# A graph network kernel: every 40th tile of gathered rows is fetched from another queue

## What is computed

```python
x = _layernorm(x + L0(...))    # msg = (x @ weight[r])[edge_type, src];  segment_sum(msg, dst)
x = _layernorm(x + L1(...))    # mean over edges of x[src], two products, row norm, batch norm, relu
x = _layernorm(x + L2(...))    # three attention layers: softmax over a node's edges, then the weighted sum
x = _layernorm(x + L3(...))    # segment_sum((x @ W)[src] * norm, dst)
```

## Time and profile before

| what | value |
|---|---|
| median of 3 runs | 6719.5 us |
| profiled execution, its span | 6723.0 us |
| a0, from barrier to barrier | 995.0 us, at 385.5 to 1380.5 |
| a1 | 987.6 us, at 1380.5 to 2368.1 |
| a5 | 994.8 us, at 5728.2 to 6723.0, the end |
| POOL busy in the three | 741.9, 740.6 and 741.0 us |
| PE busy in the three | 740.0, 764.1 and 684.0 us |
| mean of one gather on POOL | 947 to 948 ns |

### The profile page before, as it was taken

How to read it: one execution, slowest core, us unless ns; L and a number is a source line. 1 busy time by engine, 2 the same in 40 slices (tenths; PEclk the granted TensorE clock), 3 DMA queues, 4 the chain that set the end, 5 groups by cost and what they waited for, 6 DMA issues and landing times. The chain is left out here.

```text
span 6723.0 us, 99397 instructions
## 1 busy us (share of the span) xinstructions
PE 4854.4 (72%) x16882; PEld 2870.2 (43%) x16882; DVE 4480.4 (67%) x11778; ACT 2890.5 (43%) x11603; POOL 4623.8 (69%) x4896
## 2 busy tenths in 40 slices
PE   9977777777777757777775777775767767677676
PEld 4445555544444334444443444443444444343333
DVE  5145555555555578888887888886888888555554
ACT  3310000000000057888875888885788887000000
POOL 0057777767777727777766777776777776677776
PEclk9987888877777777888787888877787788767777
DMA  6444444433333345555544555554555553333333
GB/s 205 159 133 118 119 119 119 118 106 106 105 105 106 105 134 143 142 143 142 145 120 127 146 141 146 141 143 144 137 141 144 141 143 104 108 112 112 112 112 103
DMA packets 422180, 865.31 MB, mean 129 GB/s; under 512 B 104046, under 2 KB 246407, under 8 KB 421579
## 3 DMA queue, kind: packets, MB, share of 16 engines
q0 software_dynamic: 231328, 637.39, 34.9%
q1 hardware_dynamic: 151344, 184.21, 8.4%
q10 hardware_dynamic: 38906, 37.37, 1.8%
HBM read 756.50 MB, written 102.08 MB: 128 GB/s over the span
## 5 line engine op out<-in xcount | busy, mean ns | idle before, releaser
L614 POOL DMA_INDIRECT rows_a<-table,rows_src x2460 | 2354.7, 957 | 887.0 <-issue 525.9
L765 PE MATMUL ps<-rows_a,hot_a 128*128 x4992 | 1978.8, 516 | 758.9 <-DMA rows_a<-table,rows_tile_a 318.1
L1914 ACT ACTIVATE rows_a<-rows_a,ex_a 128x64 f32<-128x64 f32 x9600 | 2324.0, 337 | 0.0
L1977 PE MATMUL ps<-rows_a,hot_a 128*128 128x260 f32 x4920 | 1823.2, 491 | 155.6 <-DVE agg L1826 141.6
L712 DVE TENSOR_TENSOR agg<-agg,ps 128x256 f32 (+1 forms) x2496 | 1047.8, 420 | 1286.8 <-PE ps L765 1244.4
L765 PEld LDWEIGHTS ps<-rows_a,hot_a 128*128 128x128 f32 x4992 | 1065.6, 244 | 1587.1 <-DVE agg L712 789.5
L669 POOL DMA_INDIRECT rows_a<-table,rows_tile_a x1500 | 1421.0, 947 | 457.0 <-issue 248.0
L1826 DVE TENSOR_TENSOR agg<-agg,ps 128x260 f32 x2496 | 1039.9, 417 | 319.9 <-PE ps L1977 130.8
L1977 PEld LDWEIGHTS ps<-rows_a,hot_a 128*128 128x128 f32 x4920 | 978.6, 230 | 448.6 <-issue 341.1
L669 POOL DMA_INDIRECT rows_a<-table,row x782 | 741.7, 948 | 238.4 <-issue 131.2
L2067 ACT ACTIVATE root_a<-mv_a,eps 128x1 f32<-128x1 f32 x49 | 14.4, 295 | 976.1 <-DVE mv_a L2090 976.1
(11 more groups left out here) (338 smaller groups left out, 4144.4 us busy)
## 6 DMA issues: line engine op xcount, KB each, us to landing
dstt_a<-dloc_dram SPq DMA_DIRECT2D x156, 512.0 KB
own_a<-table SPq DMA_DIRECT2D x4608, 1.0 KB
table<-ob SPq DMA_DIRECT2D x48, 1024.0 KB, 4.4
rows_a<-table,rows_src POOLq DMA_INDIRECT x2460
rows_a<-table,rows_tile_a POOLq DMA_INDIRECT x1500, 2.8
table<-ob_n SPq DMA_DIRECT2D x98, 130.0 KB, 2.9
rows_a<-table,row POOLq DMA_INDIRECT x782, 2.8
x_dram<-cur ACTq DMA_DIRECT2D x1, 6400.0 KB
```

Of the source, the lines that this page charges most:

```text
L614: nc.gpsimd.indirect_dma_start(out=rows[:, n % ring, 0:width], out_offset=None, in_=table, in_offset=bass.IndirectOffsetOnAxis(ap=index[:, ...
L765: nc.tensor.matmul(ps[n % banks][:, 0:width], hot[:, m % nbuf, j, :], mine[n % 4], start=True, stop=True).then_inc(step_done, 1)
L1914: ins = nc.scalar.mul(a, a, ex[:, k % GV, s, h:h + 1])
L1977: nc.tensor.matmul(ps[j % banks][:, 0:W4], hot[:, j, :], step_rows(k, j), start=True, stop=True).then_inc(step_done, 1)
```

## The change

`TRING` falls from 64 to 62. Tiles 39, 79, ... 759 (every 40th, 19 of 782, `OWN_TILES`) are left out by POOL in a0, a1 and a5. SP fetches them row by row with `ask_rows`, to three more places behind the ring (62, 63, 64): 4 register loads and 128 DMAs of 1 KB a tile. It asks for a tile's byte addresses one tile ahead (two buffers, `own_index`), and before its fourth tile and each one behind it waits until the tile that had the place is used. PE waits for such a tile until all 128 DMAs have counted up `own_full`. The step table gets 12 small DVE instructions for the places, 2 for the byte addresses, and SP 2 more stores. Each stage has its own semaphores for the new waits.

```diff
-TRING = 64
+TRING = 62
 LOAD = 32
+OWN_TILE = 40
+OWN_TILES = tuple(range(OWN_TILE - 1, T - 1, OWN_TILE))
+OWN_PLACES = 3
...
                         sp.dma_start(own_src_dram, own_src[:]).then_inc(whole_out, 16)
+                        for q in range(2):
+                            sp.dma_start(own_tile_dram[q], own_tile[:, q]).then_inc(whole_out, 16)
...
+                quotient(forties, tile, OWN_TILE)
+                ch.link(nc.vector.scalar_tensor_tensor(out=mine[:], in0=forties[:], scalar=float(-OWN_TILE), in1=tile[:],
+                                                       op0=ALU.mult, op1=ALU.add))
+                ch.link(nc.vector.tensor_scalar(mine[:], mine[:], float(OWN_TILE - 1), None, ALU.is_equal))
+                quotient(place, forties, OWN_PLACES)
...
+                ch.link(nc.vector.tensor_tensor(slot_f[:], slot_f[:], place[:], ALU.add))
...
-        rows = sb(f"rows_{name}", [P, TRING, width], FP, c)
+        rows = sb(f"rows_{name}", [P, TRING + OWN_PLACES, width], FP, c)
...
                 for t in range(T):
+                    if t in OWN_TILES:
+                        continue
                     if fetch and t == TRING // 2:
                         pool.wait_ge(index_in, 16)
...
                 after.sp_first(sp)
+
+                def ask_index(i):
+                    sp.dma_start(own_index[:, i % 2], own_tile_dram[0 if with_deg else 1, :, i:i + 1].rearrange("p o -> o p"),
+                                 allow_slow_non_contiguous=True).then_inc(own_in[i % 2], 16)
+                ask_index(0)
+                for i in range(len(OWN_TILES)):
+                    if i + 1 < len(OWN_TILES):
+                        ask_index(i + 1)
+                    if i >= OWN_PLACES:
+                        sp.wait_ge(step_done, min(OWN_TILES[i - OWN_PLACES] + NB, S))
+                    sp.wait_ge(own_in[i % 2], 16 * (i // 2 + 1))
+                    ask_rows(sp, mybir.EngineType.SP, own_index[:, i % 2], 0, P, LOAD, octets, 4 * D, table.shape[0] - 1,
+                             rows[:, TRING + i % OWN_PLACES, 0:D], own_full[i % OWN_PLACES])
...
                         while landed <= tile_by(n):
-                            u, turn = landed % TRING, landed // TRING
-                            pe.wait_ge(slot_full[u], 16 * (base[u] + turn + 1))
+                            if landed in OWN_TILES:
+                                w = OWN_TILES.index(landed)
+                                pe.wait_ge(own_full[w % OWN_PLACES], 16 * P * (w // OWN_PLACES + 1))
+                            else:
+                                turns[landed % TRING] += 1
+                                pe.wait_ge(slot_full[landed % TRING], 16 * turns[landed % TRING])
                             landed += 1
```

More of the change, by code:

```diff
@@ L168, in build @@
     own_src_dram = nc.dram_tensor("own_src_dram", (P, len(OWN_BATCHES)), I32, kind="Internal").ap()
+    own_tile_dram = nc.dram_tensor("own_tile_dram", (2, P, len(OWN_TILES)), I32, kind="Internal").ap()
     src_dram = nc.dram_tensor("src_dram", (P, SP_), I32, kind="Internal").ap()
@@ L202, in steps_and_first_table @@
         odd = sb("odd", [P, SC], FP, c)
+        forties, mine, place = (sb(q, [P, SC], FP, c) for q in ("forties", "mine", "place"))
         joins = sb("joins", [P, 2, P], FP, c)
@@ L224, in steps_and_first_table @@
         own_src = sb("own_src", [P, len(OWN_BATCHES)], I32, c)
+        own_tile = sb("own_tile", [P, 2, len(OWN_TILES)], I32, c)
         (cleared, constants, made, numbered, edges_in, fields_made, edges_stored, counted, summed, edge_asked, edge_read,
@@ L336, in _ @@
                 sp.wait_ge(rows_out, 16 * (1 + H))
-                sp.wait_ge(whole_out, 96)
+                sp.wait_ge(whole_out, 128)
             @block.vector
@@ L432, in _ @@
                                                        op0=ALU.mult, op1=ALU.add))
+                quotient(forties, tile, OWN_TILE)
[3 more added lines that the diff above has]
+                quotient(place, forties, OWN_PLACES)
+                ch.link(nc.vector.scalar_tensor_tensor(out=place[:], in0=place[:], scalar=float(-OWN_PLACES), in1=forties[:],
+                                                       op0=ALU.mult, op1=ALU.add))
+                ch.link(nc.vector.scalar_tensor_tensor(out=place[:], in0=place[:], scalar=float(TRING), in1=slot_f[:],
+                                                       op0=ALU.add, op1=ALU.subtract))
+                ch.link(nc.vector.tensor_tensor(place[:], place[:], mine[:], ALU.mult))
+                ch.link(nc.vector.tensor_tensor(slot_f[:], slot_f[:], place[:], ALU.add))
                 ch.link(nc.vector.tensor_tensor(ind0[:], ind0[:], ordered[:, 0:NB].unsqueeze(1).to_broadcast([P, SC, NB]),
@@ L504, in _ @@
                                         4.0 * W4, None, ALU.mult)
+                n = len(OWN_TILES) * OWN_TILE
+                for q, a in enumerate((row0, rows_tile)):
+                    each = a[:, 0:n].rearrange("p (i e) -> p i e", e=OWN_TILE)
+                    nc.vector.tensor_scalar(own_tile[:, q], each[:, :, OWN_TILE - 1:].rearrange("p i e -> p (i e)"),
+                                            4.0 * D, None, ALU.mult)
                 nc.vector.tensor_copy(cont[:], crow.rearrange("o (k u) -> o u k", u=UG)[:, 0])
@@ L623, in build @@
     why_row = "row numbers are made from src and etype as the gathers' are"
-    why_slot = "slots are numbers modulo TRING"
+    why_slot = "slots are numbers modulo TRING, or TRING and a number modulo OWN_PLACES"
     def ask_rows(eng, of, numbers, lo, hi, load, flat, size, last, place, full):
@@ L646, in aggregate @@
         width = D + 1 if with_deg else D
-        rows = sb(f"rows_{name}", [P, TRING, width], FP, c)
+        rows = sb(f"rows_{name}", [P, TRING + OWN_PLACES, width], FP, c)
+        own_index = sb(f"own_index_{name}", [1, 2, P], I32, c)
+        octets = table.bitcast(BYTE).rearrange("r b -> (r b)")
+        own_in = [sem(f"own_in_{name}{u}") for u in range(2)]
+        own_full = [sem(f"own_full_{name}{u}") for u in range(OWN_PLACES)]
         hot = sb(f"hot_{name}", [P, nbuf, u8, P], FP, c)
@@ L653, in aggregate @@
         for j in range(TRING):
-            used[j] += len(range(j, T, TRING))
+            used[j] += sum(1 for t in range(j, T, TRING) if t not in OWN_TILES)
         count = ps[7][:, 0:P]
@@ L744, in rows_of @@
                     pe.load(regs, slots[0:1, q * 4:q * 4 + 4])
-                    views = [rows[:, bass.ds(nc.s_assert_within(pe.snap(r), 0, TRING - 1, skip_runtime_bounds_check_because=why_slot), 1),
+                    views = [rows[:, bass.ds(nc.s_assert_within(pe.snap(r), 0, TRING + OWN_PLACES - 1, skip_runtime_bounds_check_because=why_slot), 1),
                                   :].rearrange("p o w -> p (o w)") for r in regs]
@@ L749, in rows_of @@
                     return views
-                landed, ahead = 0, rows_of(0)
+                landed, ahead, turns = 0, rows_of(0), list(base)
                 for m in range(UNITS):
```

## The result

The changed kernel takes 6761.3 us (median of 4 runs) against 6720.3 us: a ratio of 1.0054, 95% interval 1.0042 to 1.0066. It is slower, by about 41 us, where 80 were forecast. The profiled execution was the quickest of the changed kernel's (6749.7 us, span 6747.9); the other three lie at 6761 to 6762. What follows is read from that profile, and so it explains the 24.9 us between the two profiled spans.

What follows compares the result with a forecast made beforehand. POOL's gather pace was taken as the bound, with SP at 51.8 us a tile replacing it. Stages lengthen by 24.8, 28.9 and 26.1 us, 79.8 in all: 6719.5 + 79.8 = 6799 us, range 6735 to 6880.

Steps and rivals of the forecast that it cites:

- What bounds the kernel before: In a0, a1 and a5, POOL's gathers, about 1.2523 us apart, set the pace and PE follows.
- What takes its place: In a0, a1 and a5, SP becomes the bound: 51.8 us a tile against POOL's 48.8 for 39 gathers.
- A: Rival: SP is hidden below 48.8 us a tile, POOL stays the bound, each stage loses 23.8 us, 6648; chance 0.08.
- B: Rival: at 50.2 to 50.6 us a tile on SP it comes out even, 6706 to 6733; chance 0.07.
- C: Rival: SP's rows are held back on their way, 80 us a tile, 8300; chance 0.08 for forms adding over 165 us.
- SP's 51.8 us for a tile: SP's work per own tile: bursts 42.16 us, four loads of 2.26, address request 0.56, wait 0.06.
- The lead-in: At each stage's start, SP's wait for its first addresses: 4 us, at most 6.8.
- What is given back at the end: After the last own tile, PE takes 22 steps at 0.80 us instead of POOL's 1.2523: 10.0 us a stage.
- the forecast's landing times of tile 759: When tile 759 landed before the change: 1340.1 in a0, 2334.6 in a1, 6681.5 in a5.
- what would show it: Signs in the new profile: bursts back to back on SP, PE waiting for own rows, POOL idle many us for PE.
- The parts put at nothing: DVE's twelve links (0, without cover 2.4 us), SP's two stores (0, at most 2.5), the ring of 62 (0).

Runs made afterwards that it cites:

- the loads of 16: Kernel with every 40th tile on SP, its addresses in 8 register loads of 16 instead of 4 of 32: 6859.6 us in a single execution.

## Why the prediction was wrong

- **What bounds the kernel before: right.** POOL's own pace. Taking 17 or 18 gathers a stage away from it, with SP hidden or nearly so, gave 60 to 65 us, where 1.2523 us each make 64 and 68.
- **What takes its place: right.** SP is slower than POOL's 48.8 us a tile; PE waits for every own tile, and SP's instructions are the chain. The rivals A, B and C did not come about: A was 1.1 to 2.6 us a tile away and holds for every 43rd and 44th; C is refuted by the 1.1 us from SP's last row to PE, and by the loads of 16.
- **The step that failed is the size of one term, SP's 51.8 us for a tile.** It was 49.9, 51.2 and 51.4 us: 19 x (1.9 + 0.6 + 0.4) = 55 us too much, and 79.8 - 55 = 25 us is the profiled execution's difference. Within the term the loads were right (a median of 2.14 against 2.18 us; a5's few long ones are what keeps its tile at 51.4). The bursts were not: 128 rows were put at 42.16 us from a2. In a0's timeline a tile's 128 rows with three loads between take 47.08 us, less 3 x (2.14 + 0.08) = 40.4; in a1 48.15 - 6.7 = 41.5. I argued that the same instructions give the same time; a2's were the slowest kind of what turned out to differ by up to 15 ns a row from stage to stage. Two per cent of the term, 1.0 us on the average, took away 55 of the 80 us, because SP's and POOL's times nearly cancel: 57 us for each us of the tile, which the text had, while the range for that us came from bursts and loads of a2 alone and stopped at 50.8. For a1 and a5 that held; for a0 it did not. The mean of the three is 50.8, the lowest that was given, and by the forecast's sum that makes 23 us. That the measured 6761 us lies well inside the stated 6735 to 6880 is partly luck: it owes 16 us to what no term of the sum accounts for, the distance of the two profiled executions from their medians.
- **The lead-in** was put at 4 us in each stage. From SP's first request to its first load it was 387.7 - 384.8 = 2.9 us in a0, 5.8 in a1 (1380.0 - 1374.2) and 3.4 in a5 (5741.2 - 5737.8): right in the sum.
- **What is given back at the end**, 10 us a stage, was right in the sum too. From PE's going on after the last own tile to the stage's end it took 33.2 us in a0, 23.1 in a1 and 28.9 in a5 (6747.9 - 6718.98; the lines of a0 and a1 stand below). With the forecast's landing times of tile 759, it had been 40.4, 33.5 and 41.5 before: 7, 10 and 13 us given back, 30 together. That the sum agrees is in part luck: 26 steps are left at that point (806 to 831), not 22, but they went quicker than the 0.80 us forecast, in a5 the first nine in 5.93 us, 0.66 each, and all in 17.7 (6736.7 - 6719.0) where 22 x 0.80 = 17.6.

```profile
1337.31 3.03 PE L813 MATMUL ps<-rows_a,hot_a 128*128 x6 [14.53 <-DMA rows_a<-table]
...
2353.71 6.32 PE L813 MATMUL ps<-rows_a,hot_a 128*128 x14 [18.31 <-DMA rows_a<-table]
```

- **A miss in what would show it.** I expected POOL to wait many us for PE. It never did in the changed kernel: its idle times put down to PE are 223.5 us in 733 times, 0.30 each. The ring was deep enough: POOL issued its last gather of a5 at 6693.0, 25 us before SP's last row. With every 36th tile it did wait, 439.2 us in 710 times, 0.62 each.

```profile
  PE ps L813: 223.5, 733
```

- **The parts put at nothing were small or nothing**: the ring by its own run; table work and stores by the start of a0, at 384.8 us in the changed kernel against 385.5 before; all of them and the places by every 43rd and 44th, where they are in and the gain is within 7 us of what POOL's gathers give.

**What stays open.** The executions other than the profiled one are longer for every 40th tile, by 12 us the first time and 6 to 31 the second, and for every 42nd by 14; for every 43rd and 44th they are not. Every 40th and 44th were measured side by side on one chip, so the chip is not the difference between those two; the gap of every 42nd can be its chip's. The pattern fits SP as the pace (0.2 us a tile more on SP makes 12 us where SP sets the time, and is hidden where it doesn't), but no trace shows those executions, so it is argued and not shown. And it isn't known what sets a row's time on SP.

## What to carry to other kernels

When work moves from the engine that sets the pace to an idle one, compare the two by the time between two hand-overs: here 39 gathers of POOL, 48.8 us, against 51 us of SP's instructions for one tile. The move pays in full as long as the idle engine stays below that, and a share that is a little smaller (every 43rd instead of every 40th) turns a loss of 0.5% into a gain of 0.9%. Where the two are close, an error of 2% in the price of one step decides over the size of the result, and in one of the three stages it decided over the sign; so the range must come from several places in the trace, not from one.

## What the hardware showed that was not expected

- The same row DMA on SP took 213 to 228 ns in the median depending on stage and program; in the changed kernel nine in ten lie within 2 ns of their stage's median. Source table, layout of the places, semaphores, the row's size (1024 or 1040 bytes) and the number of loads in a tile were changed without effect; 18 own tiles a stage, in place of 17, 19 or 21, shifted all three stages by 3 to 4 ns, not all in one direction.
- A register load of 32 addresses took 2.14 us and one of 16 took 1.24, so 16 addresses more cost 0.9 us, 0.056 us each. The straight line through these two, which leaves 0.34 us for none, was not tested at other sizes.
- Single rows of 1 KB issued every 0.31 us over a whole stage kept up with their issue: in a5 PE went on 1.1 us after the last of 2432 was issued.
